# Cross-attention and add: scores by four and three heads, plain fp32 queries, 18 slots, eight groups stored in halves

## The reference

```python
NH = 16; dk = D // NH; scale = 1.0 / np.sqrt(dk)
q = (tgt @ Wq.T).reshape(B, N, NH, dk).transpose(0, 2, 1, 3)
k = (memory @ Wk.T).reshape(B, N, NH, dk).transpose(0, 2, 1, 3)
v = (memory @ Wv.T).reshape(B, N, NH, dk).transpose(0, 2, 1, 3)
probs = jax.nn.softmax(jnp.einsum('bhqd,bhkd->bhqk', q, k) * scale, axis=-1)
att = jnp.einsum('bhqk,bhkd->bhqd', probs, v)
att = att.transpose(0, 2, 1, 3).reshape(B, N, D)
return tgt + att[0]
```

## Time and profile before

| | us |
|---|---|
| median of 3 runs | 190.33 (189.73 to 190.62) |
| profiled execution, its time | 188.74 |
| profiled execution, its span | 186.6 |
| PE, DVE, ACT, POOL busy | 127.9, 105.7, 96.3, 80.7 |
| DMA moved | 71.52 MB, 383 GB/s on average |

### The profile page before, as it was taken

One profiled execution on the slowest core, in us unless ns is written; L12 is line 12 of the kernel. 1 busy time (PEld: TensorE's weight loads), 2 busy tenths in 40 slices (PEclk: granted clock), 3 DMA queues, 4 the chain that ended last, 5 costly groups with the idle time before them and its releaser, 6 DMA issues.

```text
span 186.6 us, 3382 instructions
## 1 busy us (share of the span) xinstructions
PE 127.9 (69%) x1240; PEld 94.0 (50%) x1240; DVE 105.7 (57%) x171; ACT 96.3 (52%) x225; POOL 80.7 (43%) x45
## 2 busy tenths in 40 slices
PE   6999999999995978998889998798881000000000
PEld 6878877668663756775657666565550000000000
DVE  0455646643709999636699766945618999300000
ACT  2525535566476789679698778898860000000000
POOL 1000000000009999800099996399966999200000
PEclk9999999999999999999999999999999555555555
DMA  6999999999998999999999999999999999999996
GB/s 211 378 359 418 410 409 410 408 407 407 383 410 293 331 332 344 343 305 382 395 386 398 386 367 404 403 407 404 406 416 416 408 422 421 412 418 421 421 421 258
DMA packets 31968, 71.52 MB, mean 383 GB/s; under 512 B 1872, under 2 KB 10064, under 8 KB 31824
## 3 DMA queue, kind: packets, MB, share of 16 engines
q1 hardware_dynamic: 31952, 71.31, 99.9%
HBM read 37.75 MB, written 33.55 MB: 382 GB/s over the span
## 4 chain that ended last, share of the span: by engine, by line
PE 52%; DVE 14%; ACT 13%; issue 6%; DVEq 1%; POOL 0%; ACTq 0%; POOLq 0%
PE bank L387 12%; PE bank L367 8%; ACT probs L586 7%; PE bank L322 6%; PE bank L356 6%; PE bank L345 6%; DVE slots L719 5%; ACT probs_t L594 5%; PE bank L314 5%; PE bank L398 4%; DVE slots L709 3%; DVE neg_max L666 3%; PE bank L469 3%; DVE slots L702 1%; PE bank L409 1%
## 5 line engine op out<-in xcount | busy, mean ns | idle before, releaser
L272 POOL TENSOR_TENSOR slots<-slots,att_rows 128x512 f32<-128x512 f32 (+1 forms) x27 | 43.4, 1650 | 70.0 <-DVE att_rows L691 70.0
L586 ACT ACTIVATE probs<-bank,neg_max 128x512 f32<-128x512 f32 x64 | 44.9, 702 | 12.1 <-DVE neg_max L666 11.7
L666 DVE TENSOR_REDUCE neg_max<-bank 128x1 f32<-128x512 f32 x64 | 41.8, 682 | 11.9 <-PE bank L367 11.8
L387 PE MATMUL bank<-ident,probs 128*128 128x128 f32 x256 | 39.8, 281 | 7.8 <-ACT probs L586 6.7
L594 ACT COPY probs_t<-bank 128x512 f32<-128x512 f32 x64 | 37.7, 592 | 10.8 <-PE bank L387 10.0
L387 PEld LDWEIGHTS bank<-ident,probs 128*128 128x128 f32 x256 | 28.1, 140 | 21.3 <-ACT probs L586 17.1
L367 PE MATMUL bank<-k_t,x_q 32*128 32x512 f32 x192 | 24.1, 425 | 0.0
L278 POOL TENSOR_TENSOR slots<-slots,att_rows 128x1024 f32<-128x1024 f32 x8 | 18.6, 2377 | 4.8 <-DVE att_rows L691 4.8
L286 POOL TENSOR_TENSOR slots<-slots,att_rows 128x2048 f32<-128x2048 f32 x4 | 18.0, 4532 | 3.4 <-DVE att_rows L691 3.4
L702 DVE TENSOR_TENSOR slots<-slots,bank 128x512 f32<-128x512 f32 (+1 forms) x21 | 17.7, 856 | 0.1
L398 PE MATMUL bank<-probs_t,v 128*32 128x128 f32 x512 | 17.3, 276 | 0.7 <-ACT probs_t L594 0.7
(11 more groups left out here) (41 smaller groups left out, 98.6 us busy)
## 6 DMA issues: line engine op xcount, KB each, us to landing
slots<-in_x_dram SPq DMA_DIRECT2D x19, 1024.0 KB, 14.5
slots<-in_x_dram SPq DMA_DIRECT2D x26, 512.0 KB, 8.6
out_dram<-slots SPq DMA_DIRECT2D x13, 1024.0 KB, 14.1
out_dram<-slots SPq DMA_DIRECT2D x22, 512.0 KB, 8.7
out_dram<-slots SPq DMA_DIRECT2D x32, 256.0 KB, 3.6
ctx_raw<-in_ctx_dram SPq DMA_DIRECT2D x1, 1024.0 KB, 4.9
wq_raw<-in_L_xattn_Wq_dram SPq DMA_DIRECT2D x1, 1024.0 KB, 9.1
wv_raw<-in_L_xattn_Wv_dram SPq DMA_DIRECT2D x1, 1024.0 KB, 11.8
```

The costliest lines, as they stand in the source:

```text
L272: nc.gpsimd.tensor_tensor(xs, xs, a.unsqueeze(1).to_broadcast([P, BPS, a.shape[1]]), ALU.add).then_inc(added[g], 1)
L387: last = nc.tensor.transpose(bank[:, PT_BANK + h % 2, t * P:(t + 1) * P], probs[:, h % 2, t * P:(t + 1) * P], ident[:, :])
L586: nc.scalar.activation(probs[:, h % 2, :], bank[:, h % S_BANKS, :], ACT.Exp, bias=neg_max[:, h:h + 1], scale=1.0, accum_out=row_sum[:, h:h ...
L666: nc.vector.tensor_reduce(neg_max[:, h:h + 1], bank[:, h % S_BANKS, :], AX_X, ALU.max, negate=True).then_inc(max_ready, 1)
```

## The change

SLOTS is 18: two groups of the second half are loaded ahead. FIRST and SECOND are units of groups 0 to 7 only; groups 8 to 15 get tile 0's whole row at SECOND, added and stored in one piece. Six groups (2 to 7) of the second half are reloaded by rows, eight whole. The slots that wait for the values (14 to 17) all wait for the last value chunk; before, two of them waited for half of it. After the first four heads of a tile, scores come for three heads at once. Exponentials and turned probabilities share a ring of eight: the copy overwrites the head it came from, and head h + 8 waits for the weighing of head h's group. The query projection is plain fp32: two instructions a chunk, x and wq are not split. Tile 1's query chunks stand behind tile 0's fourth score group, and its q_t behind head 15.

```diff
@@ -29,12 +29,12 @@
     C = D // P
     HG = HEADS // HPG
     GROUPS = B // BPS
-    SLOTS = GROUPS + 1
-    PAIR = 2
-    PAIRS = HEADS // PAIR
+    SLOTS = GROUPS + 2
+    TRIPLE = 3
+    TRIPLES = (HEADS - HPG) // TRIPLE
     S_BANKS = 4
     PT_BANK, BACK_BANK, ATT_T_BANK = 4, 6, 7
-    PT_SLOTS = 6
+    RING = 8
     WARM_UP = 24
...
+    POOL_HALVED, DVE_HALVED = (1, 3, 5, 7), (0, 2, 4, 6)
+    POOL_WHOLE, DVE_WHOLE = (9, 11, 13, 15), (8, 10, 12, 14)
+
+
+    FRESH = SLOTS - GROUPS
+    BY_ROWS = range(FRESH, FRESH + 6)
+    ADDED_BY_ROWS, STORED_BY_ROWS = (0, 1, 2, 3, 4, 5, 6, 7), (0, 1, 2)
+    LAST_ROW_DVE_GROUPS = (3, 4, 5, 6, 7, 0, 1, 2)
+    WHOLE_POOL_GROUPS = (8, 10, 12, 14)
+    WHOLE_DVE_GROUPS = (9, 11, 13, 15)
+    LAST_STORE_ORDER = (3, 4, 5, 6, 7, 0, 1, 2, 8, 9, 10, 11, 12, 13, 14, 15)
     assert T == 4 and C == 4 and HG == 4 and N == 512 and D == HEADS * DK
...
+        q_t = sb("q_t", [P, 2, HG, 2, P], F32R)
+        wq_t = sb("wq_t", [P, C, D])
         k_t = sb("k_t", [P, HG, 2, N], F32R)
         v = sb("v", [P, T, D])
-        probs = sb("probs", [P, 2, N])
-        probs_t = sb("probs_t", [P, PT_SLOTS, T, P])
+
...
                 ("k_t", 0, 5), ("wk_t", 2, 0), ("wq_t", 0, 1), ("k_t", 1, 7), ("wk_t", 3, 3), ("wq_t", 1, 4),
                 ("wq_t", 2, 6), ("k_t", 2, 2), ("wq_t", 3, 7), ("x0_t", 0, 0), ("k_t", 3, 5), ("wv_t", 0, 3),
-                ("q", 0, 1), ("x0_t", 1, 4), ("wv_t", 1, 6), ("q_t", 0, 7), ("wv_t", 2, 0), ("wv_t", 3, 2),
-                ("v", 0, 6), ("v", 1, 7), ("v", 2, 6), ("v", 3, 7), ("q", 1, BACK_BANK), ("q_t", 1, ATT_T_BANK)]
+                ("q", 0, 1), ("wv_t", 1, 6), ("q_t", 0, 7), ("wv_t", 2, 0), ("x0_t", 1, 4), ("wv_t", 3, 2),
+                ("v", 0, 6), ("v", 1, 7), ("v", 2, 6), ("v", 3, 7), ("q", 1, ATT_T_BANK), ("q_t", 1, PT_BANK)]
...
-            return g if J == 0 else (g - 1) % SLOTS
+            return (J * GROUPS + g) % SLOTS
 
         def rows_of(J, g, r, cols=slice(0, D)):
             return slots[:, slot_of(J, g), :, r, cols]
 
-        def cols_of(unit):
-
-            return {FIRST: slice(0, D // 2), SECOND: slice(D // 2, D), ROW_1: slice(0, D)}[unit]
+        def cols_of(unit, g):
+
+            if g in HALVED and unit != ROW_1:
+                return slice(0, D // 2) if unit == FIRST else slice(D // 2, D)
+            return slice(0, D)
+
+        def steps(unit, g):
+
+            return unit if g in HALVED else unit - 1
+
+        def place(j, h):
+
+            return ring[:, (j * HEADS + h) % RING, :]
 
         block = stack.enter_context(nc.Block())
...
-
-            LAG = 3
-            for g in FIRST_ORDER:
+                if g == CTX_T:
+                    sp.wait_ge(bank_filled, number["v", T - 1] + 1)
+                load(0, g)
+            for g in range(FRESH):
+                load(LAST_HALF, g)
+
+            LAG, ROW_LAG = 3, 2
+            for g in HALVED:
                 store(FIRST, g)
-            for g in range(GROUPS):
+            for g in HALVED:
                 store(SECOND, g)
-            for g in range(1, BY_ROWS + 1):
-                reload_row(0, g)
+            for g in range(len(HALVED), GROUPS):
+                store(SECOND, g)
+                n = g - len(HALVED) - ROW_LAG
+                if n >= 0:
+                    reload_row(0, BY_ROWS[n])
             for g in range(GROUPS):
                 store(ROW_1, g)
-                if g >= LAG:
-                    reload(g - LAG + 1)
-            for g in range(GROUPS - LAG + 1, GROUPS):
+                if LAG - 1 <= g < GROUPS - FRESH + LAG - 1:
+                    reload(g - LAG + 1 + FRESH)
+            for g in range(GROUPS - LAG + 1 + FRESH, GROUPS):
                 reload(g)
             for g in STORED_BY_ROWS:
...
+            for unit, groups in ((FIRST, POOL_HALVED), (SECOND, POOL_HALVED + POOL_WHOLE), (ROW_1, POOL_GROUPS)):
                 pool.wait_ge(att_ready, unit)
-                a = att[:, cols_of(unit)]
-                for g in POOL_GROUPS:
+                for g in groups:
                     pool.wait_ge(loaded[0][g], 16)
-                    xs = rows_of(0, g, unit // ROW_1, cols_of(unit))
+                    a = att[:, cols_of(unit, g)]
+                    xs = rows_of(0, g, unit // ROW_1, cols_of(unit, g))
                     nc.gpsimd.tensor_tensor(xs, xs, a.unsqueeze(1).to_broadcast([P, BPS, a.shape[1]]),
                                             ALU.add).then_inc(added[g], 1)
...
+                last = mm(job_bank("q", j), x0_t[:, c, :], wq_t[:, c, :], start=(c == 0), stop=(c == C - 1))
                 if c == C - 1:
                     last.then_inc(bank_filled, 1)
 
...
-                pe.wait_ge(exp_ready, j * HEADS + pair * PAIR - PAIR)
-                scores(j, range(pair * PAIR, (pair + 1) * PAIR))
+            def score_triple(j, h):
+                pe.wait_ge(exp_ready, j * HEADS + h + TRIPLE - S_BANKS)
+                scores(j, range(h, h + TRIPLE))
 
...
+                turn_probs(j, 2)
                 if more:
                     if j + 1 == ROWS:
                         pe.wait_ge(loaded[LAST_HALF][0], 16)
                     turn("x0_t", j + 1)
-                turn_probs(j, 2)
                 turn_probs(j, 3)
-                score_pair(j, 3)
                 turn_probs(j, 4)
-                turn_probs(j, 5)
                 if more:
                     emptied(pe, "x0_t", j + 1)
                 weigh_values(j, 0)
-                score_pair(j, 4)
+                score_triple(j, 7)
+                turn_probs(j, 5)
                 turn_probs(j, 6)
                 if more:
                     pe.wait_ge(att_t_ready, j * HG + 1)
@@ -436,24 +453,22 @@
                 turn_probs(j, 7)
                 if more:
                     query_chunk(j + 1, 1)
-                score_pair(j, 5)
+                score_triple(j, 10)
                 turn_probs(j, 8)
                 if more:
                     query_chunk(j + 1, 2)
+                    query_chunk(j + 1, 3)
                 turn_probs(j, 9)
+                turn_probs(j, 10)
                 if more:
-                    query_chunk(j + 1, 3)
-                score_pair(j, 6)
-                if more:
-                    raw_queries_out(j + 1)
+                    emptied(pe, "q", j + 1)
                 weigh_values(j, 1)
-                turn_probs(j, 10)
+                score_triple(j, 13)
+                turn_probs(j, 11)
+                turn_probs(j, 12)
                 if more:
                     pe.wait_ge(att_t_ready, j * HG + 2)
                     turn_queries(j + 1)
-                turn_probs(j, 11)
-                score_pair(j, 7)
-                turn_probs(j, 12)
                 turn_probs(j, 13)
                 if more:
                     emptied(pe, "q_t", j + 1)
...
             turn_probs(0, 5)
             value_chunk(3, 1)
+            turn_probs(0, 6)
             value_chunk(3, 2)
-            turn_probs(0, 6)
-            value_chunk(3, 3)
             turn_probs(0, 7)
             score_group(0, 2)
-            query_chunk(1, 0)
+            value_chunk(3, 3)
             emptied(pe, "v", T - 1)
             weigh_values(0, 0)
-            query_chunk(1, 1)
             turn_probs(0, 8)
-            query_chunk(1, 2)
             turn_probs(0, 9)
-            query_chunk(1, 3)
             weigh_values(0, 1)
             turn_probs(0, 10)
-            raw_queries_out(1)
-            turn_back(0, range(HG // 2))
             turn_probs(0, 11)
             score_group(0, 3)
+            turn_back(0, range(HG // 2))
+            query_chunk(1, 0)
+            turn_probs(0, 12)
+            query_chunk(1, 1)
+            turn_probs(0, 13)
+            query_chunk(1, 2)
+            query_chunk(1, 3)
+            turn_probs(0, 14)
+            emptied(pe, "q", 1)
+            weigh_values(0, 2)
+            turn_probs(0, 15)
+            pe.wait_ge(probs_t_ready, HEADS - 1)
             turn_queries(1)
-            turn_probs(0, 12)
-            turn_probs(0, 13)
+            weigh_values(0, 3)
             emptied(pe, "q_t", 1)
-            weigh_values(0, 2)
-            turn_probs(0, 14)
-            turn_probs(0, 15)
             score_group(1, 0)
-            weigh_values(0, 3)
             turn_back(0, range(HG // 2, HG))
             heads(1)
             turn_back(1, before=SECOND)
...
-                    act.wait_ge(transposed, j * HEADS + h - 1)
-                nc.scalar.activation(probs[:, h % 2, :], bank[:, h % S_BANKS, :], ACT.Exp, bias=neg_max[:, h:h + 1],
+                before = j * HEADS + h - RING
+                if before >= 0:
+                    act.wait_ge(att_t_summed, before // HPG + 1)
+                nc.scalar.activation(place(j, h), bank[:, h % S_BANKS, :], ACT.Exp, bias=neg_max[:, h:h + 1],
                                      scale=1.0, accum_out=row_sum[:, h:h + 1]).then_inc(exp_ready, 1)
 
...
-
                 for h in range(HPG, HEADS):
```

(41 more changed lines are left out.)

175 lines of the change are left out of this document (73 added, 102 removed).

## The result

The changed kernel takes **200.28 us** (median of 4, 199.53 to 201.32) beside 190.03 us for the kernel before (189.71 to 190.62): a ratio of **1.054, 95% interval 1.047 to 1.061**. The prediction said slower, and that was right, but 196.9 with a range up to 200.0 was too low. A second series gave 199.75 us and 1.052 (1.046 to 1.058). In every series executions more than 1.5% above the fastest of the same kernel are in the median but not in the ratio. The profiled execution has a span of 197.8 us in a time of 199.61, against 186.6 in 188.74.

The account below looks back on a forecast made before the run. The DMA stream bounds the kernel: ROW_1's flow at 101.3 + 0.3 + 89.8 + 1.8 gives 193.2 us of span, 6.6 over 186.6; added to the median 190.33, 196.9 us. Range 192 to 200, likeliest 194 to 199 (0.58).

Parts of the forecast that it names:

- what bounds the kernel: Whole kernel: a stream of DMA transfers; a term counts only if it changes the stream's rate or leaves a hole.
- slower because work stands behind ROW_1: Stream behind the first ROW_1 store: transfers moved there raise its work from 85.0 to 89.8 us; slower at 0.86.
- both holes: Stream empty ahead of SECOND's first store for 2.7 us and ahead of ROW_1's first store for 7.0 us.
- FIRST's norm: First half of tile 0's attention: first normalisation at 56.6 us, against 55.84 before.
- tile 1's scores: Tile 1's first scores, waiting for both parts of q_t: at 65.45 us, against 63.63 before.
- the wait of query chunk 0 for VectorE's copy: Tile 1: TensorE free from 77.95, but att_t group 0's copy, behind a maximum and whole-row add, ends at 79.4.
- the chunk itself: Plain fp32 query chunk on TensorE: taken as 0.9 us, between bounds of 0.27 and 1.08.
- The hole at 57: Stream gap at 57 to 59 us before: goes, as the first store flows at 59.75, before the loads are through.
- The ring or the triples bring nothing because their waits bind elsewhere: Rival, every tile: another 1.5 us or more a tile, giving 199 us and up; chance 0.08 (later still).
- the triples' saved 1.8 us: TensorE in tile 1: four score sets of 0.9 us where there were six save 1.8 us, which goes into waits.
- Tile 1: Step from SECOND's to ROW_1's normalisation: first weighing at 75.3, second at 86.45, normalisation at 97.7 us against 92.99.
- Behind ROW_1 0.3 + 89.8 + 1.8: Stream after ROW_1's stores flow: 0.3 us for row order, 89.8 of transfers, 1.8 empty in the last slice.

Follow-up runs that it names:

- the idle transposes: Changed kernel with idle TensorE transposes of resident data ahead of tile 1's heads 0 and 1 and head 4's score triple; 198.43 us, 1.048.
- pairs and early queries: Changed kernel with scores in pairs and tile 1's queries where the kernel before has them, its stream plan kept; 192.68 us, 1.015.
- the old plan in the changed kernel: Changed kernel with the stream order of the kernel before: all sixteen groups in halves, twelve rows loaded again; 195.62 us, 1.033.
- the run with the adds behind the even heads: Changed kernel with VectorE's additions of SECOND and later behind the even heads' maxima instead of the odd ones'; 198.07 us, 1.050.
- the plan alone: Kernel before, computation and 17 slots kept, with the change's stream order: groups 0 to 7 in halves, six rows loaded again; 195.76 us, 1.029.
- the kernel with early queries: Changed kernel with tile 1's query projections and scores' turns put back ahead of tile 0's last scores; 195.35 us, 1.031.

## Why the prediction was wrong, step by step

Right: what bounds the kernel; slower because work stands behind ROW_1; both holes, at 67.0 to 69.9 and about 95.5 to 103.6 (2.9 and 8.1 us, where 2.7 and 7.0 were forecast); FIRST's norm 56.99 (56.6), SECOND's 67.53 (67.05), tile 1's scores 65.90 (65.45); the wait of query chunk 0 for VectorE's copy, 1.09 us (1.45); the chunk itself, 1.02 us where nothing delays it (0.9). The hole at 57 went. "The ring or the triples bring nothing because their waits bind elsewhere" at 0.08 was the rival nearest to the result: triples do cost 1.1 to 1.7 us a tile against pairs, and the time is above its 199. That the triples' saved 1.8 us would just go into waits was too mild: the waits grew by more than that.

Two terms were mis-sized. First **"Tile 1"**: SECOND's norm to ROW_1's was to be 30.65 us (67.05 to 97.7) and was 32.57. Of these 1.9 us the granted clock is 1.4, shown by the idle transposes. The prediction had the chain that makes TensorE wait (maxima and adds in turn on VectorE), and left every duration as it was at 2.4 GHz. So the first weighing came at 77.33, not 75.3, which is 9.8 us behind SECOND's norm instead of 8.25; with the clock kept up it is 8.3. Behind it the forecast holds: to the second weighing 11.3 us for 11.15, to ROW_1's norm 22.8 for 22.4. With 0.5 us from SECOND this is 2.4 us at ROW_1.

Second **"Behind ROW_1 0.3 + 89.8 + 1.8"**: from the norm to the end 95.5 us were forecast and 97.7 measured. The first 12 us behind the first ROW_1 store were to move 4.3 MB (10.7 us at 401 GB/s, after 1.3 of start) and moved 3.9 (12 at 324): 1.0 us. The tail cost 3.3 us and not 1.8 (4.6 us at 116 of 419 GB/s; 2.4 in the second profile, so it varies): 1.5. The middle was 0.3 us quicker than forecast. A dry stretch ahead of ROW_1 does not explain the two by itself. With pairs and early queries the stream moved 305 GB/s in the 6 us ahead of its first ROW_1 store (91.2 to 97.2) and 326 in the 12 us behind it; all runs with the new plan have 320 to 328 there, those with the old plan in the changed kernel 339 to 358. And the run with the adds behind the even heads has the same hole and a full tail, 261 GB/s in its last 4.6 us. The cause of either stays open.

Together: 2.4 us at ROW_1 and 2.2 us behind it, so 193.2 of span became 197.8. The median moved by less than the span, since the profiled execution of before lay 1.6 us under its median and that of after 0.7.

## What to carry to other kernels

In a kernel bound by its stream, count the bytes that stand behind each release point (an event that lets stores or loads go), and take the norm's time in the new kernel, not in the old one. Here the plan alone put 1.4 MB behind ROW_1's norm, which cost more than larger pieces gave back. Lateness was paid in full once the stream was dry: putting the queries back brought ROW_1's norm forward by 4.7 us and the time down by 4.4 to 4.9. Where a forecast itself shows TensorE waiting again and again, price the work behind the waits at either clock. Less work on an engine that waits is no gain by itself: look for the partner it catches up with.

## What the hardware showed that was not expected

After 67 to 70 us with 0.90 us of work, in pieces a microsecond apart, the granted clock was 0.51 in 70 to 76 us although TensorE was then busy 5.45 of 6 us; in the kernel with early queries it had 1.34, 1.50 and 1.03 us of work in the three 2 us windows from 66 to 72 and the clock stayed at 1.0.

In these runs the stream lost about a microsecond where the first loads joined a stretch of stores alone; no run shows why. In the changed kernel, with the DMA engines shown busy, it happens at the first row reloads,

```profile
79.00:82.00 3.00, 1.91 (x16) 1.20 (x11) 2.65 (x5) 1.74 (x4) 3.00 (x2) 1.00 1.00 267
```

and again at ROW_1's first reloads, the 287 GB/s in 107 to 111 above. The kernel before, which moved 391 GB/s in the 6 us ahead of ROW_1's first store, has 385 in 103 to 107. Moving the reloads in the kernel before moved the dip from 82 to 84 us to 77 to 79 and did not remove it.
